# Moving the value products of an attention group next to their exponentials, and reordering the score units

## What is computed

```python
def _attention_mc(x, Wq, Wk, Wv, Wo):            # layer 1, head size 8
    q, k = _rope(q), _rope(k)
    scores = jnp.einsum('bhqd,bhkd->bhqk', q, k) * scale
    scores = jnp.where(causal, scores, jnp.finfo(scores.dtype).min)
    attn = jax.nn.softmax(scores, axis=-1)
    out = jnp.einsum('bhqk,bhkd->bhqd', attn, v)
    return out.transpose(0, 2, 1, 3).reshape(B, S, D) @ Wo.T
...
    x = x + _layernorm(_L0_attn_ref(_layernorm(x), Wq, Wk, Wv, Wo))
    x = x + _layernorm(_L0_ffn_ref(_layernorm(x), ...))
    # inside _L0_ffn_ref (layer 2, latent keys shared by the heads):
        x = x + _attention(_rmsnorm(x, w_ln1), Wq, Wkva, Wkvb, Wo)
        return x + _moe(_rmsnorm(x, w_ln2), Wgate, expert_bias, Wg, Wu, Wd, sWg, sWu, sWd)
```

## Time and profile before

| | |
|---|---|
| median of 3 runs | 644.71 us (642.79 to 644.81) |
| profiled execution | 640.79 us, its span 638.8 us |
| PE busy | 541.8 us (85%) |
| DVE, ACT, POOL busy | 398.9, 307.2, 209.2 us |
| mean granted TensorE clock | 0.954 |

### The profile page before, as it was taken

The page is one execution under the profiler, slowest core; times in us unless marked ns, Lnnn a source line. Parts: engine busy times, 40 slices in busy tenths (PEclk is TensorE's granted clock), DMA queues, the critical chain, the costliest instruction groups (busy, mean ns, idle before and its releaser), DMA issues.

```text
span 638.8 us, 9915 instructions
## 1 busy us (share of the span) xinstructions
PE 541.8 (85%) x3538; PEld 300.5 (47%) x3538; DVE 398.9 (62%) x942; ACT 307.2 (48%) x585; POOL 209.2 (33%) x273
## 2 busy tenths in 40 slices
PE   3569989888877997799878998989999998899872
PEld 1424435433444554444435555545575456643632
DVE  6588787667757554566755576756556765435463
ACT  1314666664557643456526545644445532564221
POOL 4372454333625522650442311424231110220011
PEclk9976999999889897799979999999999999999987
DMA  9660214113353450201570122216304120000000
GB/s 227 179 178 13 65 47 151 40 40 104 127 106 84 132 164 21 100 35 66 102 198 36 58 49 51 51 68 150 76 10 96 22 52 2 18 2 1 1 17 16
DMA packets 29488, 47.19 MB, mean 74 GB/s; under 512 B 4608, under 2 KB 15104, under 8 KB 28928
## 3 DMA queue, kind: packets, MB, share of 16 engines
q1 hardware_dynamic: 28480, 46.01, 27.0%
q10 hardware_dynamic: 960, 0.56, 0.4%
HBM read 27.22 MB, written 18.87 MB: 72 GB/s over the span
## 4 chain that ended last, share of the span: by engine, by line
PE 58%; DVE 20%; ACT 6%; issue 5%; POOL 4%; SPq 3%; DMA 3%; POOLq 0%; DVEq 0%; ACTq 0%
PE ps L571 12%; PE ps L528 9%; PE ps L634 8%; DVE NM L1144 6%; PE ps L499 6%; PE ps L496 4%; PE ps L501 4%; PE ps L522 3%; DVE terms L1248 2%; PE ps L756 2%; DVE stats L1128 2%; PE ps L578 2%; PE ps L682 2%; PE ps L617 1%; DVE KS L1401 1%
## 5 line engine op out<-in xcount | busy, mean ns | idle before, releaser
L1144 DVE TENSOR_REDUCE NM<-ps 128x1 f32<-128x512 f32 (+3 forms) x352 | 219.3, 638 | 118.7 <-PE ps L501 111.8
L797 ACT ACTIVATE PG<-ps 128x512 f32<-128x512 f32 x320 | 181.4, 596 | 161.2 <-PE ps L528 94.2
L528 PE MATMUL ps<-QS,K 128*128 128x512 f32 x320 | 119.4, 458 | 0.0
L501 PE MATMUL ps<-maskb,identb 128*128 128x128 bf16 x512 | 111.3, 236 | 0.0
L571 PE MATMUL ps<-PG,V 128*32 128x512 f32 (+3 forms) x1024 | 97.7, 455 | 6.9 <-POOL PG L1090 5.2
L499 PE MATMUL ps<-K,QS 96*128 96x256 f32 (+3 forms) x256 | 84.7, 375 | 15.2 <-DVE NM L1144 14.9
L496 PE MATMUL ps<-KS,QS 96*128 96x256 bf16 (+3 forms) x256 | 74.8, 328 | 20.0 <-DVE NM L1144 18.6
L501 PEld LDWEIGHTS ps<-maskb,identb 128*128 128x128 bf16 x512 | 52.8, 103 | 38.7 <-issue 31.3
L528 PEld LDWEIGHTS ps<-QS,K 128*128 128x128 f32 x320 | 51.9, 196 | 38.8 <-issue 20.3
L522 PE MATMUL ps<-QS,KS 128*128 128x128 bf16 (+3 forms) x256 | 63.9, 312 | 4.7 <-DMA QS<-scr 4.2
L988 POOL TENSOR_TENSOR rstd<-ve,half 128x4 f32<-128x4 f32 x20 | 20.5, 1023 | 139.8 <-DVE ve L1136 104.1
(11 more groups left out here) (159 smaller groups left out, 640.7 us busy)
## 6 DMA issues: line engine op xcount, KB each, us to landing
scr<-QC SPq DMA_DIRECT2D x24, 512.0 KB, 2.8
QS<-scr SPq DMA_DIRECT2D x64, 128.0 KB
scr<-room SPq DMA_DIRECT2D x20, 256.0 KB, 2.5
QS<-scr SPq DMA_DIRECT2D x16, 288.0 KB
KS<-scr SPq DMA_DIRECT2D x16, 288.0 KB
QS<-scr SPq DMA_DIRECT2D x64, 64.0 KB
x<-in_x SPq DMA_DIRECT2D x4, 256.0 KB, 5.2
out_x<-x SPq DMA_DIRECT2D x4, 256.0 KB, 2.3
```

The costliest lines, as they stand in the source:

```text
L501: return pe.matmul(dst[:, P * (k - 1):P * k], identb[:], maskb[:, 0, :], start=False, stop=True)
L528: mm = pe.matmul(bank.rearrange("p (h q) -> p h q", h=HG), keys[:, SEQ[n] % 2, P * j:P * j + P], QS2[:, heads, P * i:P * i + P], start=(ke ...
L797: act.activation(PG[:, n % 2, unit_place(LAYER[n], (u + k) % UNITS), :], ps[:, ST0 + (u + k) % 3, :], ACT.Exp, scale=scale).then_inc(exp_d ...
L1144: dve.tensor_reduce(dst, src, AX.X, ALU.max, negate=True).then_inc(fill_read, 1)
```

## The change

Group n's value products now run at (n,3) behind the fourth fill (key tile 0), (n+1,0) behind the second fill (key tile 1), and (n+1,1) behind the first and second fill (the other two; in layer 1 key tile 3 goes before 2). Each waits for as many exponentials as it needs (4, 8, 8 and 10 in layer 1; 4, 7, 9 and 10 in layer 2) and for its own mask. For this the units are computed key tile by key tile. The copy, the turn and the division each move one slot forward (ACT: slot 1 in place of 2; PE: the end of slot 2 in place of 3; DVE: slot (n+1,3) in place of (n+2,0)). POOL does the first mask (two in layer 2) in (n,3) and the rest in (n+1,0); before, layer 1 had all four in (n+1,0) and layer 2 all four in (n,2). No beside stage moves, and no operation is added or taken away; one clearing on POOL at the start now waits for the first mask.

```diff
--- before.py
+++ after.py
@@ -36,21 +36,20 @@
 TWO_ONES = 1.0 + 0x3F80 / 2.0 ** 23
 NEG = -1e30
 FILLS = 11
-VALUES_AT = ((1, 0), (1, 1), (1, 2), (2, 0))
+VALUES_AT = ((3, 3), (0, 1), (1, 0), (1, 1))
 UNITS = 10
 
-CAUSAL_ORDER = (0, 1, 2, 3)
-
-BLOCKS2 = ((0, 0), (1, 1), (2, 2), (3, 3), (0, 1), (0, 2), (0, 3), (1, 2), (1, 3), (2, 3))
+VALUE_ORDER = {1: (0, 1, 3, 2), 2: (0, 1, 2, 3)}
+VALUE_UNITS = {1: (4, 8, 8, 10), 2: (4, 7, 9, 10)}
+
+BLOCKS2 = ((0, 0), (0, 1), (0, 2), (0, 3), (1, 1), (1, 2), (1, 3), (2, 2), (2, 3), (3, 3))
 PLACE2 = (0, 4, 7, 9)
 
...
@@ -531,7 +530,6 @@
 
             def scores_for_exp(n, hh, i):
 
-                h = HG * (n % G) + hh
                 u = n * UNITS + 5 * (hh // 2) + 2 * (hh % 2) + i
                 if hh == 0 and i == 0:
                     pe.wait_ge(m_stacked[n % G], 16 * (n // G + 1))
@@ -541,17 +539,19 @@
                 if LAYER[n] == 2:
                     mm = scores_t2(bank, n, *BLOCKS2[u % UNITS])
                 else:
-                    tiles = (((0, T, h, 0),), ((0, 3 * P, h, 1), (3 * P, T, h, 3)),
-                             ((0, 256, h - 1, 2), (256, T, h, 2)))[i]
+                    c, h = u % UNITS, HG * (n % G)
+                    tiles = (((0, T, h + c, 0),), ((0, 3 * P, h + c - HG, 1), (3 * P, T, h + c - HG, 3)),
+                             ((0, 256, h + 2 * c - 16, 2), (256, T, h + 2 * c - 15, 2)))[c // HG]
                     for lo, hi, head, j in tiles:
                         mm = scores_t1(bank[:, lo:hi], head, j)
                 mm.then_inc(st_ready, 1)
 
-            def values(n, j):
-
-                pe.wait_ge(causal, NT * (n + 1) if LAYER[n] == 2 else NT * n + CAUSAL_ORDER.index(j) + 1)
-                if j == 0:
-                    pe.wait_ge(exp_done, UNITS * (n + 1))
+            def values(n, k):
+
+                j = VALUE_ORDER[LAYER[n]][k]
+                pe.wait_ge(exp_done, UNITS * n + VALUE_UNITS[LAYER[n]][k])
+                pe.wait_ge(causal, NT * n + k + 1)
+                if k == 0:
...
-                    mm = pe.matmul(out, v, p, start=(j == 0), stop=(j == NT - 1), skip_group_check=True)
-                if j == NT - 1:
+                    mm = pe.matmul(out, v, p, start=(k == 0), stop=(k == NT - 1), skip_group_check=True)
+                if k == NT - 1:
                     mm.then_inc(pv, 1)
 
             def turn_out(n):
@@ -595,9 +595,11 @@
                         scores_for_exp(n, hh, i)
                     if n + 2 < NG and i < fills_of(hh)[1]:
                         scores_for_max(n + 2, hh, i)
-                    if 1 <= n <= NG and (hh, i) in VALUES_AT:
-                        values(n - 1, VALUES_AT.index((hh, i)))
-                if hh == 3 and 1 <= n <= NG:
+                    if (hh, i) in VALUES_AT:
+                        k = VALUES_AT.index((hh, i))
+                        if 0 <= n - (k > 0) < NG:
+                            values(n - (k > 0), k)
+                if hh == 2 and 1 <= n <= NG:
                     turn_out(n - 1)
 
             def bank(u):
@@ -796,7 +798,7 @@
                         act.wait_ge(st_ready, u + k + 1)
                         act.activation(PG[:, n % 2, unit_place(LAYER[n], (u + k) % UNITS), :], ps[:, ST0 + (u + k) % 3, :],
                                        ACT.Exp, scale=scale).then_inc(exp_done, 1)
-                if hh == 2 and 1 <= n <= NG:
+                if hh == 1 and 1 <= n <= NG:
                     act.wait_ge(pv, n)
                     if n >= 2:
                         act.wait_ge(o_turned, n - 1)
...
@@ -1080,28 +1084,35 @@
                 pool.wait_ge(q_low, c + 1)
                 pool.sem_inc(job_done[j], 1)
 
-            def causal_blocks1(n):
+            def causal_blocks1(n, order):
                 pair = PG[:, n % 2, 0:8, :].rearrange("p (h k) t -> p h k t", k=2)
                 both = PG[:, n % 2, 8:10, :].rearrange("p a (b t) -> p a b t", b=2)
-                pool.wait_ge(exp_done, UNITS * (n + 1))
-                for j in CAUSAL_ORDER:
+                for k in order:
+                    j = VALUE_ORDER[1][k]
+                    pool.wait_ge(exp_done, UNITS * n + VALUE_UNITS[1][k])
                     blocks = (pair[:, :, 0, 0:P], pair[:, :, 1, 0:P], both[:, :, :, 0:P], pair[:, :, 1, 3 * P:T])[j]
                     heads = [[0, 2], [0, 2]] if j == 2 else [[0, HG]]
                     pool.affine_select(blocks, blocks, pattern=[*heads, [1, P]], compare_op=ALU.is_ge, fill=0.0, base=0,
                                        channel_multiplier=-1).then_inc(causal, 1)
 
-            def causal_blocks2(n):
-                for c in range(NT):
-                    blocks = PG[:, n % 2, unit_place(2, c), :].rearrange("p (h q) -> p h q", h=HG)
-                    pool.wait_ge(exp_done, UNITS * n + c + 1)
+            def causal_blocks2(n, order):
+                for c in order:
+                    blocks = PG[:, n % 2, PLACE2[c], :].rearrange("p (h q) -> p h q", h=HG)
+                    pool.wait_ge(exp_done, UNITS * n + PLACE2[c] + 1)
                     pool.affine_select(blocks, blocks, pattern=[[0, HG], [1, P]], compare_op=ALU.is_ge, fill=0.0, base=0,
                                        channel_multiplier=-1).then_inc(causal, 1)
 
             def main(n, hh):
-                if hh == 0 and 1 <= n <= NG and LAYER[n - 1] == 1:
-                    causal_blocks1(n - 1)
-                if hh == 2 and 0 <= n < NG and LAYER[n] == 2:
-                    causal_blocks2(n)
+                if hh == 0 and 1 <= n <= NG:
+                    if LAYER[n - 1] == 1:
+                        causal_blocks1(n - 1, (1, 2, 3))
+                    else:
+                        causal_blocks2(n - 1, (2, 3))
+                if hh == 3 and 0 <= n < NG:
+                    if LAYER[n] == 1:
+                        causal_blocks1(n, (0,))
+                    else:
+                        causal_blocks2(n, (0, 1))
 
...
@@ -1196,12 +1207,12 @@
                    .then_inc(on_ready, 1)
 
             def main(n, hh):
-                split, out = hh == 0 and 0 <= n + 1 < NG, hh == 0 and 2 <= n <= NG + 1
+                split, out = hh == 0 and 0 <= n + 1 < NG, hh == 3 and 1 <= n <= NG
                 for i in range(4):
                     if split:
                         split_max(n + 1, i)
                     if out and i < 2:
-                        divide(n - 2, i)
+                        divide(n - 1, i)
                     if n + 2 < NG and i < 2 + hh % 2 + hh // 3:
                         maximum(n + 2, hh, i)
```

10 lines of the change are left out of this document (5 added, 5 removed).

## The result

The changed kernel takes 654.85 us (median of 4, 651.62 to 655.22), the kernel before 644.28 beside it: ratio 1.0159, interval 1.0122 to 1.0196. Repeated later with others on one chip, it took 653.3 against 642.7, ratio 1.0154 (1.0101 to 1.0208). The forecast of 640.6 was wrong, and so was its range. The profiled execution took 655.22 us, its span is 653.3.

A forecast was written before the change was run, and what follows sets the result against it. PE's work and its holes bound the kernel, and only holes change: -4.5 - 3.3 - 2.4 + 4.3 + 1.8 + 1.0 - 1.0 = -4.1 us, so 640.6 for the median; range 634.5 to 648.5.

The forecast's parts named there:

- What bounds the kernel: PE, busy 542 of 639 us, and its holes bound the kernel; its work stays the same, only holes can change.
- The clock: Two new holes of over 2 us may each bring half clock, +1.6 each; left out of the sum, +-3 in range.
- Slots 0 and 1 (-4.5): Value products cover six fills' waits for DVE (3.4 us); three first products' waits for the division (1.6) go: -4.5.
- Division one slot earlier (-3.3): `o1T` and `o2T` no longer wait for the division; at the end its 0.90 and the copy's 0.3 go: -3.3.
- Value products moved into or out of a hole (-2.4): Group 10's transfer wait -0.6, two waits for masks -0.8, group 13's hole -1.0.
- the -0.8 for masks: Two waits for POOL's masks, caused by `parts1` and `ropeB` work ahead of them, shrink: together -0.8.
- First mask behind lna2 (+4.3): Groups 6 and 14: first mask stands behind POOL's norm chain, so key tile 0's value product waits: 2.0 and 2.3.
- Cover lost in slots 1 and 2, and slot 3 (+1.8, +1.0, -1.0): Lost cover in three layer-1 groups +1.8; late POOL `parts1`, `parts1b` in groups 2 and 3 +1.0; slot 3 -1.0.
- extreme of slot 3: Division ahead of DVE's slot-3 reductions against PE's turn, over 16 groups: at best -7, at worst +8.
- POOL holds the value product in slot 3: Rival, chance 0.18: at (n,3,3) POOL late by 0.7 us in eight groups (+5.6), slow clock +3.2: 649 to 650.
- my two conditions for being wrong: PE's waits for POOL grow by over 6 us in sum, or those for DVE don't fall.
- DVE and POOL in each other's way: Rival, chance 0.05: layer 2's masks in slot 0 slow DVE's splits there, costing 3 us: 643 to 645.

The follow-up runs named there:

- the clock held: Idle products (results unread) fill PE's long waits: kernel before 636.55 us, ratio 0.9948; changed kernel 640.44 us, ratio 0.9955.
- mask_slot2_idle2: Changed kernel with the first mask (two in layer 2) in POOL's slot 2 and idle products in long holes: 633.86 us, 0.9844 of before.
- after_idle2: Changed kernel with idle products in long holes, group 10's ahead of the wait for group 12's queries: 640.44 us, 0.9955 of before.
- before_idle2: Kernel before with idle products in 14 long holes, group 10's ahead of the wait for group 12's queries: 636.55 us, 0.9948 of before.
- values_late: Changed kernel with value products, copy, turn and division back at their old slots, units and masks as changed: 640.77 us, 0.9960 of before.
- before_idle: Kernel before with idle products in 14 long waits, group 10's 60 behind the transfer wait, not ahead of it: 642.79 us, 0.9998 of before.

## Why the forecast was wrong, step by step

**What bounds the kernel.** "The work is the same before and after, product for product, so only the holes can change": this is the step that failed. The products are the same, their time is not. In the stretch compared above PE's idle time fell by 2.0 us, and its busy time rose by 12.2.

The sum of the holes failed too, by less. With the clock held the stretch is 1.3 us longer (468.22 less 466.90), where the whole sum gave -4.1. The start and the tail, for which the sum had +1.0 and -1.2, grew by 4.3 us together in the two profiles as they are. No term was there for groups 15, 23, 24 and 30, which with the clock held take 0.4, 0.5, 0.6 and 0.4 us more.

**The clock.** I left it out of the sum and gave it +-3 us, by counting new holes of over 2 us. It was the largest term: the difference between the two kernels is 1.59% as they are and 0.07% with the clock held (0.9955 less 0.9948). That would be nearly the whole 10.6 us; with up to +4 us left over (above) it is some 6 us at the least, and in the stretch it is 8.9 of 10.2. The kernel before already paid for it (6.1 us of its stretch), which I read off one row and not as a sum. The rule that I quoted from the Trainium skill (TensorE: Matmul & The Clock Gate, section HAM oscillation), that idle gaps in a loop bring the half rate back, pointed the right way. The section's own case is a loop with longer waits than these, so it gave no measure for them; I applied it to two holes of over 2 us, and the profile shows the lower clock behind 1.2 to 1.6 us as well.

**Slots 0 and 1 (-4.5).** Right for layer 1. With the clock held, groups 4, 5 and 6 take 11.40, 12.24 and, in mask_slot2_idle2, 11.17 us, against 11.85, 12.71 and 11.72: 0.5 us each. In the changed profile only one first fill of slot 1 still waits for DVE, but part of the gain went elsewhere. In group 22 the 0.96 us for the division became 0.76 for a mask, and in group 29 1.33 us became 0.42 for DVE and, a few lines later, 0.52 for a mask:

```profile
552.34 0.50 PE L498 MATMUL ps<-K,QS 96*128 96x512 f32 x1 [0.42 <-DVE NM L1155]
...
553.43 0.42 PE L571 MATMUL ps<-PG,V 128*32 128x256 f32 x4 [0.52 <-POOL PG L1102]
```

**Division one slot earlier (-3.3).** Right at group 21: 19.74 us in place of 21.40. Wrong at the end, where I had counted -0.9 and -0.3. DVE had an experts' operation first, and the wait grew from 0.90 to 1.72:

```profile
604.59 0.69 DVE L1428 TENSOR_TENSOR QS<-QS,ps 128x512 f32<-128x512 f32 x1 [0.48 <-PE ps L636]
...
605.71 0.42 DVE L1205 TENSOR_TENSOR room<-ps,rec 128x256 f32<-128x256 f32 x1
...
606.19 1.11 PE L719 MATMUL ps<-ident_sb,room 128*128 128x128 f32 x4 [1.72 <-DVE room L1205]
```

**Value products moved into or out of a hole (-2.4).** With the clock held, groups 9 to 11 took 47.12 us before and 46.19 in after_idle2: -0.9, about my -0.6 and the half of the -0.8 for masks that belonged to group 10. Group 13 went from 26.12 to 24.11, -2.0 for -1.0 here and -0.4 in the division's term. The other half of the masks came out on the other side. In group 18 key tile 1's product now waits 2.48 us, 0.5 more than the 1.94 that key tile 0's waited before:

```profile
334.40 1.26 POOL L1082 TENSOR_TENSOR QC<-whole,QC 128x512 fp32r<-128x512 f32 x1 [3.73 <-ACT QC L899]
...
336.61 1.51 PE L571 MATMUL ps<-PG,V 128*32 128x384 f32 x8 [2.48 <-POOL PG L1095]
```

Group 18 as a whole took 18.48 us before and 21.41 after, but its windows show that this is PE's busy time and not its waits, 4.5 and 4.6 us:

```profile
328.65:347.14 18.49, 13.99 (x107) 8.31 (x107) 9.45 (x24) 8.01 (x17) 7.58 (x10) 0.91 0.37 112
```

```profile
334.22:355.63 21.41, 16.81 (x108) 9.18 (x108) 10.31 (x28) 8.28 (x16) 7.78 (x10) 0.78 0.31 97
```

With the idle products it took 18.52 and 21.36 us. The clock wasn't held there, though: after_idle2 has an unfilled wait of 2.35 us for ACT's queue (0.90 in before_idle2), and the lower clock behind it.

```profile
335.67 0.66 PE L730 MATMUL ps<-ident_sb,room 128*128 128x128 f32 x4 [2.35 <-ACTq L832]
...
336.80:340.10 3.30, 3.30 (x18) 2.93 (x16) 1.25 (x2) 1.28 (x3) 0.00 (x0) 0.50 0.02 7
```

values_late takes 21.41 us in this group as well, with a wait of 4.33 us at the same transposes, and its value products stand at the old places. So the loss here need not come from them; which part of the change brings it isn't shown.

**First mask behind lna2 (+4.3).** The holes came as forecast, 2.43 and 2.30 us. With the clock held groups 6 and 14 take 13.67 and 15.89 us in after_idle2, and 11.17 and 14.32 in mask_slot2_idle2: 4.1 us, close to the term. The move of the mask is worth more than these two groups: 6.3 us of the stretch with the clock held and 8.2 without (483.18 to 474.99). Group 18 has 1.9 of the 6.3 (21.36 to 19.44).

**Cover lost in slots 1 and 2, and slot 3 (+1.8, +1.0, -1.0).** These small terms weren't tried by themselves; the profiles show the first two. The waits for DVE at the third fill of slot 1 were 1.09, 0.10 and 0.69 us in groups 10, 17 and 27 and are 0.53, 2.01 and 0.53 in groups 8, 10 and 17: +1.2 for the +1.8. Groups 2 and 3 take 0.8 us more each, +1.6 for the +1.0. The holes of slot 3's third fill grew by 0.1 us (1.12 to 1.21, 1.30 to 1.39, 1.91 to 2.02), so neither extreme of slot 3 happened.

**The rivals.** The nearest was "POOL holds the value product in slot 3", 649 to 650, and its measure, over 6 us more of PE's waits for POOL, was missed only just (+5). Its place was right in the `lna2` groups, but all other groups showed no wait of over 0.3 us at (n,3,3) but for two (0.51 and 1.22), which the profile puts down to ACT. It had the clock at 3.2 us, the same error as the forecast. Of my two conditions for being wrong neither was met (DVE's waits at the fills did fall, by 0.7 us), and I was wrong: both looked only at holes. "DVE and POOL in each other's way" didn't happen: DVE is busy for 396.1 in place of 398.9 us, and the first split takes 0.175 us at the median of 16 and at most 1.36, where it took 0.176 and 1.59.

## What to carry to other kernels

Where PE has holes, its busy time isn't a constant of the program: compare it between two profiles first, then the granted clock over the same stretch of work, and only then the holes. A forecast for a kernel with holes of over 1 us needs a term for the lower clock of the size of all its slow stretches: here a rearrangement took them from 30.7 to 51.2 us. And where work is placed right behind its producer, look for the one queue that now holds it back: here the first mask moved by one slot on POOL was worth 1.0%.

Putting idle products into long waits is a cheap way to take the clock out of a comparison, and here it paid by itself: 0.5% for the kernel before (its interval nearly reaches 0), 2.0% for the changed one. They must stand ahead of the very wait in which the time passes, as before_idle shows.

## What the runs showed of the hardware

The lower clock costs less than its length: between group 4 and 31 filling the holes took 20.5 us of it from the kernel before (30.7 to 10.2 us, read from the granted clock of the profile) for 6.1 us of time, and 44.4 us (51.2 to 6.8) from the changed one for 15.0, a third of a us for each us. The price isn't one number, though: from the kernel before to the changed one 20.5 us more of it came with 10.2 us more time. Holes of 1.1 to 2.0 us were followed by it in one layout in most cases and in another in few, at lengths that differ by 0.1 us. In the changed kernel it was steady: both profiles have it behind the same five holes, in executions of 655.2 and 656.8 us, each the slowest of its four.
